# Softmax of two attention heads at a time, in a fused attention and feed-forward layer

## The reference

```python
y = layernorm(x)
q, k, v = y @ Wq + bq, y @ Wk + bk, y @ Wv + bv      # 8 heads, blocks of 64
scores = einsum('bnqhd,bnkhd->bhnqk', q, k) * 128 ** -0.5
x = x + einsum('bhnqk,bnkhd->bnqhd', softmax(scores), v) @ Wo + bo
h = square(relu(layernorm(x) @ W_fc.T))
y = h @ W_proj.T
mem, spk = 0, 0                                       # 5 steps
reset = mem > 1;  mem = 0.9 * mem + y - reset;  spk += mem > 1
x = x + spk / 5
```

## Time and profile before

| | |
|---|---|
| device time, median of 3 runs | 1166.43 us (1164.36 to 1166.81) |
| the profiled execution | 1161.1 us |
| its span, slowest core (core 1) | 1159.5 us |
| spans of all cores | 1142.8 to 1159.5 us |
| busy share of the span | PE 72%, PE weight load 52%, DVE 42%, ACT 35%, POOL 22% |
| chain that ended last | PE 58%, DMA 18%, DVE 9%, ACT 6%, issue 5% |

### The profile page before, as it was taken

How to read it: one execution, slowest core, us unless ns; L and a number is a source line. 1 busy time by engine, 2 the same in 40 slices (tenths; PEclk the granted TensorE clock), 3 DMA queues, 4 the chain that set the end, 5 groups by cost and what they waited for, 6 DMA issues and landing times.

```text
span 1159.5 us, 19231 instructions; the slowest of 8 cores (1142.8 to 1159.5 us)
## 1 busy us (share of the span) xinstructions
PE 836.2 (72%) x6624; PEld 604.8 (52%) x6624; DVE 491.5 (42%) x561; ACT 411.0 (35%) x873; POOL 254.5 (22%) x122
## 2 busy tenths in 40 slices
PE   0295369844995389638797979979798897979910
PEld 0143234332343234334686867868587686868800
DVE  0105330244104430443204828366491854839186
ACT  3131413142232414121444454444444444454400
POOL 3000000011000100000003506245161633506154
PEclk9997569955996579858798998989999899999965
DMA  9995660067103740076495959879596895959600
GB/s 160 198 235 93 140 119 1 1 114 146 32 1 73 128 92 1 10 145 206 122 310 173 297 171 310 274 217 323 172 316 209 277 323 185 317 172 332 231 36 37
DMA packets 127292, 194.21 MB, mean 167 GB/s; under 512 B 42208, under 2 KB 44256, under 8 KB 127200
## 3 DMA queue, kind: packets, MB, share of 16 engines
q1 hardware_dynamic: 108144, 151.03, 42.7%
q0 software_dynamic: 14448, 33.56, 16.1%
q10 hardware_dynamic: 4608, 8.39, 2.0%
HBM read 192.95 MB, written 25.17 MB: 188 GB/s over the span
## 4 chain that ended last, share of the span: by engine, by line
PE 58%; DMA 18%; DVE 9%; ACT 6%; issue 5%; SPq 1%; POOL 1%; DVEq 0%; ACTq 0%; POOLq 0%
PE psC L805 16%; PE psA L839 9%; PE psB L839 8%; DMA w2scratch<-w2stage 7%; DMA w1slab<-w1scratch 6%; PE psA L610 3%; DMA bv_sb<-bv 3%; PE psA L329 3%; PE psB L610 3%; PE psB L368 2%; PE psB L329 2%; PE psA L368 2%; PE psB L349 2%; PE psA L349 2%; DVE mem_q L910 2%
## 5 line engine op out<-in xcount | busy, mean ns | idle before, releaser
L805 PE MATMUL psC<-xn2t_sb,w1slab 128*128 128x256 bf16 x2048 | 277.1, 281 | 16.2 <-ACT xn2t_sb L743 11.7
L805 PEld LDWEIGHTS psC<-xn2t_sb,w1slab 128*128 128x128 bf16 x2048 | 205.3, 101 | 48.5 <-issue 19.7
L816 ACT ACTIVATE h_bf<-psC 128x256 bf16<-128x256 f32 x256 | 97.8, 382 | 222.9 <-PE psC L805 222.9
L839 PE MATMUL psA<-h_bf,w2slab 128*128 128x256 bf16 x1024 | 154.8, 274 | 24.2 <-ACT h_bf L819 22.3
L906 POOL TENSOR_TENSOR acc_q<-acc_q,spk_q 128x2048 bf16<-128x2048 bf16 (+1 forms) x27 | 148.4, 5495 | 72.4 <-DVE spk_q L902 72.4
L839 PE MATMUL psB<-h_bf,w2slab 128*128 128x256 bf16 x1024 | 154.6, 274 | 0.0
L910 DVE SCALAR_TENSOR_TENSOR mem_q<-mem_q,y_sb 128x2048 f32<-128x2048 f32 (+1 forms) x27 | 142.8, 5290 | 2.8
L839 PEld LDWEIGHTS psA<-h_bf,w2slab 128*128 128x128 bf16 x1024 | 98.5, 98 | 43.9 <-issue 32.3
L819 ACT ACTIVATE h_bf<-h_bf 128x256 bf16<-128x256 bf16 x256 | 106.6, 416 | 24.6 <-ACT h_bf L816 1.5
L839 PEld LDWEIGHTS psB<-h_bf,w2slab 128*128 128x128 bf16 x1024 | 100.8, 98 | 12.2
L218 POOL DMA_DIRECT2D wtmp<-Wfc x32 | 17.1, 538 | 394.2 <-PE psC L398 355.8
(11 more groups left out here) (98 smaller groups left out, 1044.8 us busy)
## 6 DMA issues: line engine op xcount, KB each, us to landing
w2slab<-w2scratch SPq DMA_DIRECT2D x128, 512.0 KB, 6.6
w1slab<-w1scratch SPq DMA_DIRECT2D x128, 512.0 KB, 7.5
x_sb<-x SPq DMA_DIRECT2D x4, 2048.0 KB, 43.2
wtmp<-Wpr POOLq DMA_DIRECT2D x16, 512.0 KB, 6.6
wtmp<-Wfc POOLq DMA_DIRECT2D x32, 256.0 KB, 7.3
w2scratch<-w2stage SPq DMA_DIRECT2D x32, 256.0 KB, 5.1
w1scratch<-w2stage ACTq DMA_DIRECT2D x32, 256.0 KB, 5.4
out<-x_sb POOLq DMA_DIRECT2D x16, 512.0 KB, 8.1
```

The lines of the kernel that those rows point to most:

```text
L805: op("pe", lambda E, fc=fc, c=c, hp=hp, s1b=s1b: E.matmul(hp, s1b[:, c * 128:(c + 1) * 128], xn2t_sb[:, c * 256:(c + 1) * 256], start=(c = ...
L816: op("se", lambda E, fc=fc, hp=hp: E.activation(h_bf[fc % 2][:], hp, ACT.Relu), inc="se")
L839: E.matmul(tgt[:, mc * 256:(mc + 1) * 256], slb[:, m * 128:(m + 1) * 128], h_bf[fp % 2][:], start=(fp == 0 and m % 2 == 0), stop=(fp == 31 ...
```

## The change

The softmax chain now works on a pair of heads u (heads 2u and 2u + 1). Every DVE and ACT instruction of it covers 512 elements in place of 256, there are half as many, and `p_bf` becomes one tile without a double. The 4 transposes of a pair's probabilities wait for both halves of psD, and one ACT copy takes them all out.

The loop over heads becomes a loop over pairs. Within it the steps are emitted pair by pair, and so the weight groups change their order: before, w2, w1, w2, w1 for two heads; now w2, w2, w1, w1. The layer norm pieces move with them: `ln1_part1` runs 1, 2 and 1 times after pairs 0, 1 and 2, `ln1_part2` after pair 2 and `ln1_part3` after pair 3. The bodies of `w1_group` and `w2_group` are as they were.

```diff
-        def softmax_pre(h, E_s):
+        def softmax_pre(u, E_s):
...
-                negmax[:, :4], g3, AX.X, ALU.max, negate=True), inc="ve")
+                nm3, sc4, AX.X, ALU.max, negate=True), inc="ve")
...
-        def pt_h(h):
-            wait("pe", "ve", E_p[h])
-            pe_wait_rel(relD[h % 2])
+        def pt_u(u):
+            wait("pe", "ve", E_p[u])
+            pe_wait_rel(relD[0])
+            pe_wait_rel(relD[1])
...
+        def ptev_u(u):
+            wait("se", "pe", E_pt[u])
...
+            relD[0] = ("se", n["se"])
+            relD[1] = ("se", n["se"])
...
-        for h in range(8):
-            if h + 2 < 8:
-                E_s = scores(h + 2)
-                softmax_pre(h + 2, E_s)
-                exp_h(h + 2)
-            if h + 1 < 8:
-                softmax_post(h + 1)
-                pt_h(h + 1)
-                ptev_h(h + 1)
-            pv_h(h)
-            attnev_h(h)
-            ci = 4 * p + h // 2
-            if h % 2 == 0:
-                wait("pe", *E_ld2[ci])
-            w2_group(ci, h % 2)
-            fcw = 8 * p + h
-            wait("pe", *E_w1ld[fcw])
-            w1_group(fcw)
+        for u in range(4):
+            if u + 2 < 4:
+                scores(2 * u + 4)
+                E_sb = scores(2 * u + 5)
+                softmax_pre(u + 2, E_sb)
+                exp_u(u + 2)
+            if u + 1 < 4:
+                softmax_post(u + 1)
+                pt_u(u + 1)
+                ptev_u(u + 1)
+            pv_h(2 * u)
+            pv_h(2 * u + 1)
+            attnev_h(2 * u)
+            attnev_h(2 * u + 1)
+            ci = 4 * p + u
+            wait("pe", *E_ld2[ci])
+            w2_group(ci, 0)
+            w2_group(ci, 1)
+            for dfc in range(2):
+                fcw = 8 * p + 2 * u + dfc
+                wait("pe", *E_w1ld[fcw])
+                w1_group(fcw)
             if p + 1 < PA:
-                if 1 <= h <= 4:
-                    ln1_part1(p + 1, h - 1)
-                elif h == 5:
+                if u == 0:
+                    ln1_part1(p + 1, 0)
+                elif u == 1:
+                    ln1_part1(p + 1, 1)
+                    ln1_part1(p + 1, 2)
+                elif u == 2:
+                    ln1_part1(p + 1, 3)
                     ln1_part2(p + 1)
-                elif h == 6:
+                elif u == 3:
                     ln1_part3(p + 1)
```

More of the change, by code:

```diff
@@ L60, in build_nc @@
     attn_sb = regC.enter_context(nc.sbuf_tensor("attn_sb", [128, 4096], BF16))
-    s_f32 = [e(nc.sbuf_tensor(f"s_f32_{i}", [128, 256], F32, side="right"))
-             for i in range(2)]
-    p_bf = [e(nc.sbuf_tensor(f"p_bf_{i}", [128, 256], BF16, side="right"))
-            for i in range(2)]
-    pt_bf = [e(nc.sbuf_tensor(f"pt_bf_{i}", [128, 256], BF16, side="right"))
-             for i in range(2)]
+    s2_f32 = [e(nc.sbuf_tensor(f"s2_f32_{i}", [128, 512], F32, side="right"))
+              for i in range(2)]
+    p2_bf = e(nc.sbuf_tensor("p2_bf", [128, 512], BF16, side="right"))
+    pt2_bf = [e(nc.sbuf_tensor(f"pt2_bf_{i}", [128, 512], BF16, side="right"))
+              for i in range(2)]
     ident = e(nc.sbuf_tensor("ident", [128, 128], BF16, side="right"))
@@ L381, in build_nc, with s4_of @@
         E_v_all = n["ve"]
-        E_tta = [0] * 8
-        E_p = [0] * 8
-        E_exph = [0] * 8
-        E_ptev = [0] * 8
-        E_pt = [0] * 8
+        E_tta = [0] * 4
+        E_p = [0] * 4
+        E_exph = [0] * 4
+        E_ptev = [0] * 4
+        E_pt = [0] * 4
         E_pv = [0] * 8
         E_attnev = [0] * 8
+        sc4 = bass.AP(psC[:].tensor, 0, [[1024, 128], [512, 2], [64, 4],
+                                         [1, 64]])
+        nm3 = negmax[:].rearrange("p (a g) -> p a g", a=2)
+        sm3 = ssum[:].rearrange("p (a g) -> p a g", a=2)
+        rs3 = rsum[:].rearrange("p (a g) -> p a g", a=2)
+        def s4_of(u):
+            return bass.AP(s2_f32[u % 2][:].tensor, 0,
+                           [[512, 128], [256, 2], [64, 4], [1, 64]])
         def scores(h):
             wait("pe", "se", max(E_qe[h], E_ke[h]))
-            if h >= 2:
-                wait("pe", "ve", E_tta[h - 2])
+            u = h // 2
+            if u >= 1:
+                wait("pe", "ve", E_tta[u - 1])
             else:
@@ L436, in softmax_post @@
+        def softmax_post(u):
+            wait("ve", "se", E_exph[u])
+            wait("ve", "ve", war["p"])
+            if u >= 1:
+                wait("ve", "pe", E_pt[u - 1])
+            op("ve", lambda E, u=u: E.tensor_reduce(
+                sm3, s4_of(u), AX.X, ALU.add), inc="ve")
             wait("ve", "ve", n["ve"])
-            op("ve", lambda E: E.reciprocal(rsum[:, :4], ssum[:, :4]),
-               inc="ve")
+            op("ve", lambda E: E.reciprocal(rsum[:], ssum[:]), inc="ve")
@@ L443, in softmax_post @@
                 ALU.mult), inc="ve")
-            E_p[h] = n["ve"]
+            E_p[u] = n["ve"]
             war["p"] = n["ve"]
-        def pt_h(h):
-            wait("pe", "ve", E_p[h])
-            pe_wait_rel(relD[h % 2])
-            base = (h % 2) * 1024
-            for t_ in range(2):
-                op("pe", lambda E, h=h, t_=t_, base=base: E.transpose(
-                    psD[:, base + t_ * 128:base + (t_ + 1) * 128],
-                    p_bf[h % 2][:, t_ * 128:(t_ + 1) * 128], ident[:]),
-                    inc="pe" if t_ == 1 else None)
-            E_pt[h] = n["pe"]
@@ L458, in ptev_h @@
-        def ptev_h(h):
-            wait("se", "pe", E_pt[h])
-            base = (h % 2) * 1024
-            op("se", lambda E, h=h, base=base: E.copy(
-                pt_bf[h % 2][:], psD[:, base:base + 256]), inc="se")
-            E_ptev[h] = n["se"]
-            relD[h % 2] = ("se", n["se"])
+        def pt_u(u):
+            wait("pe", "ve", E_p[u])
+            pe_wait_rel(relD[0])
+            pe_wait_rel(relD[1])
+            for q in range(2):
+                for t_ in range(2):
+                    op("pe", lambda E, q=q, t_=t_: E.transpose(
+                        psD[:, q * 1024 + t_ * 128:q * 1024 + (t_ + 1) * 128],
+                        p2_bf[:, q * 256 + t_ * 128:q * 256 + (t_ + 1) * 128],
+                        ident[:]),
+                        inc="pe" if (q == 1 and t_ == 1) else None)
+            E_pt[u] = n["pe"]
@@ L466, in pv_h @@
         def pv_h(h):
-            wait("pe", "se", E_ptev[h])
+            u = h // 2
+            wait("pe", "se", E_ptev[u])
             if h < 2:
@@ new lines, in build_nc @@
+        E_sb = scores(1)
+        softmax_pre(0, E_sb)
+        exp_u(0)
+        scores(2)
+        E_sb = scores(3)
+        softmax_pre(1, E_sb)
+        exp_u(1)
+        softmax_post(0)
+        pt_u(0)
+        ptev_u(0)
+        for u in range(4):
[20 more added lines that the diff above has]
+                w1_group(fcw)
+            if p + 1 < PA:
+                if u == 0:
[5 more added lines that the diff above has]
+                    ln1_part1(p + 1, 3)
```

72 lines of the change are left out of this document (33 added, 39 removed).

## The result

The changed kernel takes 1216.57 us (median, 1214.32 to 1223.12) against 1164.47 us of the kernel before: 1.0455 times as long, with a 95% interval of 1.0431 to 1.0478. That is +52 us. The forecast was +42 us, 1209, in a range of 1182 to 1228: slower as foreseen, by somewhat more.

What follows compares the result with a forecast made beforehand. The prediction took the head loops to be bound by latencies in a chain, its longest link the waits for stores. Terms 24 + 18 + 0 gave +42 us on 1161.1, so 1203, or 1209 for the median; range 1182 to 1228.

Steps and rivals of the forecast that it cites:

- The period: Head loops, first three blocks: time between successive pairs' first w2 copies, claimed 18.5, 20.1 and 18.9 us.
- L: Head loops: time from a pair's first w2 copy start to landing of its second w2 store, taken as 10.3 us.
- The signs named: New profile: ACT waits over 80 us for w2 stores, copies 18 to 20 us apart, second stores landing in 9 to 11.
- the 24 us: First three blocks, first w2 copy to projection: added cost of 7.0 + 8.6 + 8.6 us.
- 11 links: The times L enters the sum: three pairs in each of three blocks, two pairs in the fourth.
- The fourth block: Last head loop, no layer norm, loads only in its first half: 42.5 us against 42.6 before, cost 0.
- The start of a block: First DVE step to first w2 copy in each head loop: 12.8 us against 8.3, +4.5 per block, 18 for four.
- the DVE saving: Softmax chain: fewer, longer DVE instructions save some 0.8 us per pair, 12 us over 16 pairs, not counted as gain.
- The stalled projection: Rival: `ln1_part3`, late on DVE, delays the projection's additions; 3.4 us in each of three blocks, +10, 1219; chance 0.14.
- Early stores: Rival: second w2 stores under load land in 4.5 us, making the kernel faster, 1152 us; chance 0.08.
- cancel: Rival: ACT's wait existed before, the 12 us DVE saving reaches the end, L is 7.5: no change, 1166; chance 0.04.
- the 9.3 us of one row: Profile before, second head loop: landing time of a store issued 0.4 us after a 512 KB load, against 4.5 without.

## Why the prediction was right, point by point

**The cause.** The prediction put the loss on ACT's w1 copies waiting for w2 stores of the same pair, with the layer norm pieces, the exponential and the probability copy behind them. The timeline shows each of these in that order, and the experiments confirm it from three sides: the order alone makes it (+74 us), the old order undoes it (+2 us in place of +52), and taking the loads off the stores undoes it too (-5 us). In the last two the later start (+20 us) is still there; the rest of the loop is shorter than before (182.4 and 166.2 us in four blocks against 193.6), so they also give back time that the kernel before lost to its stores.

**The period.** Forecast 18.5, 20.1 and 18.9 us for the three pairs with L = 10.3. Core 1 of the kernel after has its w2 copies at 249.38, 268.03, 288.21 and 307.28: 18.7, 20.2 and 19.1, with L of 10.4 to 10.6. In that loop the working held to 0.2 us per period. In the first block, where L was 10.7 to 11.2, the same core's periods were 19.1, 20.3 and 19.7.

**The signs named.** ACT waits 170 us for w2 stores (over 80 named), w2 copies stand 18.3 to 20.4 us apart on core 1 and 18.7 to 22.0 on core 4 in the first three blocks (18 to 20 named), and the second stores of the pairs under load land in 9.7 to 13.4 us over all cores (9 to 11 named). The feed-forward stage is as long as before, within 2.3 us. One sign was incomplete: PE's w2 transposes (L550) wait for the probability copy as said, 24.0 us, but for the w1 copy as well, 34.2 us, at the fourth pair of a block, where there is no probability copy left.

**The mis-sized terms.** The number came out 10 us too low (+42 against +52), and the most of it lies in the 24 us. From the first w2 copy to the projection the forecast had 60.2 us for each of three blocks and 42.5 for the fourth, 223.1 in all, against 199.0 taken for before. In the mean over the cores it measured 228.8 against 193.6, +35.2. The first reason is L: over the eight cores and 11 links it was 10.9 in the mean, not 10.3; 11 times 0.6 is 6.6 us, about the 5.7 by which 228.8 exceeds 223.1. The second is the base: the rows before were those of core 1, which had the longest of the eight (197.9), and its third block was 50.5 where 51.6 was assumed. So L, which the prediction priced at 7 us between 10.3 and 10.9, is about half of the miss, and the one core's base the other half.

On core 4, the slowest of the profiled execution, the second stores of the first two blocks land in 11.7 to 13.0 us, and the periods of the second loop are 20.8, 21.9 and 20.2; in its third and fourth blocks they land in 10.3 to 10.8, as elsewhere. From first w2 copy to projection it takes 65.7, 65.4, 60.7 and 42.3 us, against 50.1, 50.2, 48.9 and 41.7 on the same core before. The fourth block cost about 1 us in the mean (43.1 against 42.1), where none was forecast.

**The start of a block.** Forecast +4.5 us each, 18 in all. Measured in the mean over the cores: 57.5 us from the first scores to the first w2 copy in four blocks in place of 37.4, so +20. From the first DVE step (243.52) it is 13.4, where 12 to 13 were named. The size was right. But I called it a cost of pairing, and the runs show it to be mainly one of standing behind the second head: with single heads and the new order it is 54.3.

**What the change removes.** I left the DVE saving out of the sum since DVE was idle half of the time. Within the sum this was harmless, as the periods were built from the new kernel's own steps. As a view of pairing it was wrong: in the chain of one pair the fewer, longer steps do count, 7 us per block without the groups and 21 us in all under the new order. Going by single heads first, the change is a loss of 74 us from the order and a gain of 21 from the pairs; going by pairs first, it is +2 and then +51. The two steps do not add up independently. My sum of two losses of 24 and 18 told neither apart; it came near because the new periods were added up from the new kernel's own steps, in which both are contained.

**Slips in the working.** By the prediction's own sum L = 9 gives 1194 us and L = 6.5 gives 1167, where it has 1192 and 1170. The range does not depend on it.

**The rivals.** The stalled projection did not come in the changed kernel:

```profile
322.33 3.62 PE L636 MATMUL psA<-wo_sb,attn_sb 128*128 128x512 bf16 x8
...
326.15 2.98 DVE L282 TENSOR_SCALAR xn_bf<-x_sb,nmean,rstd 128x1024 bf16<-128x1024 f32 x4 [5.03 <-ACT w2stage L534]
...
329.05 1.28 DVE L652 SCALAR_TENSOR_TENSOR x_sb<-psA,x_sb 128x512 f32<-128x512 f32 x2
```

Pair 3 has its 512 KB load out early, its second store lands in 3.3 us, and the additions start 6.7 us after the projection, not later than the 7.1 of the earlier trace rows. In the mean over cores and the first three blocks, the next block's transposes come 18.2 us after the projection, against 19.1 before. The stall did come in the kernel with the layer norm pieces moved. Early stores: the first of each pair was early (3.3 us), the second was not. When it was made so by holding the loads, the kernel became faster than the one before, as that rival said, but by less: 5 us, where the rival had 14. It did not cancel.

**The sharing of the DMA engines.** The prediction weighed the 9.3 us of one row against 10.9, the whole burst of loads. The second store ends with the loads beside it: on core 4 at 271.3 us, half a microsecond after the last load (270.8), and before the change at 266.5, after a load that landed at 265.9. With the loads held back it took 4.4 us. The Trainium skill, page "DMA: Bandwidth & Descriptors", section "Queues, rings and completion order", says that the engines alternate between queues that have work. By that rule the second store ends about when the loads do, and the trace agrees: 10.9 in the mean over the cores.

## What to carry to other kernels

When a loop's steps are regrouped, follow the shared resources that are handed out by a counter: here two staging tiles that had each served one engine came to serve two, and each engine's copy now waited for the other's transfer made a moment before. A wait in an in-order queue costs its own length and puts in series what used to run beside it, so ask what stands behind it. And before giving an instruction saving to a kernel, give the transfers room: loads issued when no store is being waited for took 58 us off the changed kernel, and another staging pair 61 (with two w1 buffers fewer), where the old order took 51. Look at the start of each loop as well: work that stands behind the second head's steps comes 5 us later in every block, whatever the transfers do.

## What was not expected of the hardware

The same 256 KB store took 9.7 to 13.4 us to land when the three loads went out beside it (eight cores of the changed kernel, 11 links each), and 2.9 to 7.1 us, 4.1 in the mean, with the loads held back (second store of the first three pairs in the first three blocks, eight cores).

It matters which store is waited for. Beside the same loads, the first w1 stores of the pairs in core 4's second loop landed in 7.3 to 8.1 us where the second w2 stores took 11.7 to 12.7. The w2 stores leave in pieces of 256 bytes (2080 packets for 0.52 MB in that queue from 257 to 275 us), the w1 stores in larger ones (281 packets for 0.51 MB), and they are also issued later. No run separates the two causes. So a part of what the new order costs may be that ACT now waits for the kind of store in small pieces; this was not tested.

The landing time also differs between cores for the same program: in the second loop of the changed kernel 10.4 to 10.6 us on core 1 and 11.7 to 12.7 on core 4. It is no fixed trait of a core. In the third block core 4 is back at 10.3 to 10.8, cores 3 and 5 had 12.1 to 13.4 in the first block, and in the nine counted executions the slowest core was core 2 three times, cores 4 and 7 twice, and cores 0 and 1 once each.
